# Two further, unread TensorE products per group ahead of the third layer in a message-passing kernel

## The reference

```
h = silu(rbf @ fc_w1 / sqrt(8))          # 8 -> 64
h = silu(h @ fc_w2 / sqrt(64))           # 64 -> 64
weight = h @ fc_w3 / sqrt(64)            # 64 -> 128, split into w00, w01, w10, w11
gs, gv = l1_s[edge_src], l1_v[edge_src]  # rows of a linear map of the source node
o00 = w00 * gs * sh0
o01 = w01[:, :, None] * gs[:, :, None] * sh1[:, None, :]
o10 = w10[:, :, None] * gv * sh0[:, :, None]
o11 = w11 * (einsum('ecm,em->ec', gv, sh1) / sqrt(3))
agg = segment_sum(message, edge_dst) / count
out = x + sc + tanh(alpha) * (agg @ lin2)
```

## Time and profile before

| | before |
|---|---|
| median of 3 runs | 2496.71 us |
| lowest and highest run | 2487.68 and 2497.35 us |
| span of the profiled execution | 2483.8 us |
| PE busy | 1811.4 us, 73% |
| DVE busy | 1783.0 us, 72% |
| POOL busy | 1578.4 us, 64% |
| ACT busy | 1199.1 us, 48% |
| mean granted TensorE clock | 0.826 |

### The profile page before, as it was taken

One profiled execution on the slowest core, in us unless ns is written; L12 is line 12 of the kernel. 1 busy time (PEld: TensorE's weight loads), 2 busy tenths in 40 slices (PEclk: granted clock), 3 DMA queues, 4 the chain that ended last, 5 costly groups with the idle time before them and its releaser, 6 DMA issues. The chain is left out here.

```text
span 2483.8 us, 34021 instructions
## 1 busy us (share of the span) xinstructions
PE 1811.4 (73%) x7969; PEld 1174.2 (47%) x7969; DVE 1783.0 (72%) x4669; ACT 1199.1 (48%) x3310; POOL 1578.4 (64%) x1624
## 2 busy tenths in 40 slices
PE   6577777787777777767677767667787776877777
PEld 6344444454444444444444434444554444544544
DVE  8577767767776777767676667767677776777777
ACT  6354545455454555444444344445444444445443
POOL 7566666666666666666666666666666666666563
PEclk9588878878888887788787878888888888888889
DMA  7322222222222222222122222222222222222222
GB/s 214 70 64 67 56 64 66 66 56 66 66 59 62 67 65 56 55 48 50 46 50 48 48 48 49 54 50 64 57 67 62 59 65 66 53 64 61 59 66 55
DMA packets 347699, 155.73 MB, mean 63 GB/s; under 512 B 237983, under 2 KB 322048, under 8 KB 347584
## 3 DMA queue, kind: packets, MB, share of 16 engines
q0 software_dynamic: 50016, 102.51, 15.7%
q1 hardware_dynamic: 296938, 51.75, 11.4%
q10 hardware_dynamic: 630, 0.29, 0.0%
HBM read 134.27 MB, written 20.15 MB: 62 GB/s over the span
## 5 line engine op out<-in xcount | busy, mean ns | idle before, releaser
L970 POOL DMA_INDIRECT lin_g<-lin_table,src_ix x1563 | 1530.0, 979 | 865.1 <-issue 441.5
L1157 ACT ACTIVATE lin_sh<-lin_g,harm 128x128 f32<-128x128 f32 x1563 | 483.8, 396 | 94.6 <-DMA lin_g<-lin_table,src_ix 87.6
L1040 PE MATMUL ps_sums<-near_sums,far_hot 128*128 128x257 f32 x520 | 208.0, 488 | 440.8 <-DVE agg L1474 206.0
L1030 PE MATMUL ps_near<-msg,onehot 128*64 128x257 f32 x3126 | 507.5, 471 | 1.2 <-DVE msg L1423 1.2
L1018 PE MATMUL ps_w<-w,h 128*128 128x256 f32 x1566 | 462.6, 440 | 28.2 <-ACT key_all L1167 18.5
L1018 PEld LDWEIGHTS ps_w<-w,h 128*128 128x128 f32 x1566 | 395.3, 272 | 135.4 <-issue 44.9
L999 PE MATMUL ps_h<-rbf,w 32*128 32x192 f32 x1044 | 277.0, 390 | 138.0 <-issue 67.1
L1415 DVE TENSOR_TENSOR msg<-lin_sh,key_all 128x576 f32<-128x576 f32 (+1 forms) x261 | 197.3, 756 | 249.9 <-ACT key_all L1167 209.5
L1167 ACT ACTIVATE key_all<-ps_w 128x768 f32<-128x768 f32 x261 | 213.5, 818 | 305.2 <-remote 188.6
L1030 PEld LDWEIGHTS ps_near<-msg,onehot 128*64 128x64 f32 x3126 | 241.3, 164 | 230.6 <-issue 175.7
L1383 DVE TENSOR_TENSOR lin_sh<-lin_g,ps_meta 128x576 f32<-128x576 f32 (+1 forms) x261 | 196.6, 753 | 212.2 <-DMA lin_g<-lin_table,src_ix 207.0
(11 more groups left out here) (175 smaller groups left out, 1655.2 us busy)
## 6 DMA issues: line engine op xcount, KB each, us to landing
lin_g<-lin_table,src_ix POOLq DMA_INDIRECT x1563
dist_in<-in_edge_weight SPq DMA_DIRECT2D x67, 96.0 KB
lin_table<-lin_out SPq DMA_DIRECT2D x24, 256.0 KB, 2.6
x_in<-in_x SPq DMA_DIRECT2D x24, 256.0 KB
skip_table<-x_in SPq DMA_DIRECT2D x24, 256.0 KB
xq<-in_x SPq DMA_DIRECT2D x23, 256.0 KB, 3.9
harm<-in_edge_attr SPq DMA_DIRECT2D x66, 48.0 KB
x_in<-skip_table SPq DMA_DIRECT2D x8, 256.0 KB
```

The source lines that it names most:

```text
L970: pool.indirect_dma_start(slot_tiles(s, u)[rows, t, :], None, lin_table, bass.IndirectOffsetOnAxis(ap=src_ix[rows, s.phase, u, col:col + 1 ...
L1030: mm = pe.matmul(ps_near[half * NEAR:(half + 1) * NEAR, 0:MSG + 1], onehot[:, u, t, :], msg[:, u % 2, t, :], start=(j == 0), stop=(j == PA ...
L1040: pe.matmul(ps_nodes(i), far_hot[:, u, :], near_sums[:, u % 2, :], start=True, stop=True).then_inc(sums_ready, 1)
L1157: last = act.activation(lin_sh0[:, u % 2, j, :], slot_tiles(s, u)[:, j, :], ACT.Copy, scale=harm[:, s.phase, u, harm_col(j):harm_col(j) + 1])
```

## The change

Each call of `layer3` issues two more products ahead of its own three, behind the wait for `w_copied`. Their stationary operand is `w2`, their moving operand all 256 columns of `w3`, and they write columns 768 to 1023 of `ps_w`, which nothing reads. They signal no semaphore. In the changed file the new products stand at L1018, and each later line is up to three further down (layer 3's own products L1021, `near_layer` L1033, `segment_sum` L1043).

```
+WARM = 2
...
                             at_least(pe, w_copied, i * SLOTS + u)
+                            for _ in range(WARM):
+                                pe.matmul(ps_w[:, TILES * P:], w2[:], w3[:], start=True, stop=True)
                             cols = h2[:, u % 2, :].rearrange("p (c j) -> p j c", j=PAIRS)
                             for j in range(PAIRS):
                                 mm = pe.matmul(ps_w[:, 2 * j * P:(2 * j + 2) * P], cols[:, j, :], w3[:], start=True, stop=True)
```

## The result

| | before | after |
|---|---|---|
| median | 2496.42 us | 2540.54 us |
| lowest and highest run | 2487.68, 2497.35 us | 2530.16, 2550.09 us |
| profiled span | 2483.8 us | 2540.1 us |
| mean granted clock | 0.826 | 0.864 |

The ratio is 1.018 (95% interval 1.0147 to 1.0213): slower, 44 us by the medians and 56.3 us by the two profiled spans. The forecast was 2531 us, slower by 1.4%. The medians are of four runs each.

A forecast was written before the change was run, and what follows sets the result against it. It took POOL's gathers and their waits, mostly for late TensorE messages, as the bound. Span 2483.8 plus 34 us gave 2518 us; with 12.9 us from span to median, 2531 us, range 2470 to 2630 us.

The forecast's parts named there:

- POOL's waits as the kernel's time: POOL's gathers: 1530.0 us busy plus 865.1 us idle fill nearly the whole span, so a wait there is kernel time.
- The new rows: TensorE ahead of layer 3: 4 matmul rows a call, 1044 in all, 1.18 us a group, 308 us.
- The size of the cost: Whole loop: half the upper reading for the added TensorE time, 0.13 us a group, 34 us.
- the upper slope: Loop phases with extra TensorE work: 0.14 to 0.22 us of period per added us, 43 to 68 us over 261 groups.
- the phases of the earlier trace: Three stretches of the loop before: 9.06 us a group plain, 9.13 and 9.30 with 0.49 and 1.08 us extra TensorE work.
- The clock: TensorE's mean granted clock would rise from 0.826 to 0.84 to 0.90, without making the kernel faster.
- The waits: POOL's waits for TensorE, 408 us, would grow by about 34 us; TensorE's idle before the sums would shrink, PE exceed 80% busy.
- remote: POOL's 155 waits, 325.1 us, counted as waiting for TensorE, whose messages arrived late and as POOL paused.
- "issue" pauses: POOL's 1347 short pauses of 0.33 us, 441.5 us, the cost of starting the next gather.
- The idle time before the sums: TensorE idle 440.8 us before L1040; the new products would fill 100 to 250 us of it.
- The rival "exposed": DVE's 113 waits at L1415 for ACT's copy each grow 1.18 us: 133 us, 2630 us in all; chance 0.14.
- The rival "hidden": New products end inside TensorE's idle time before L1040, POOL's waits stay: 2490 to 2509 us; chance 0.22.

The follow-up runs named there:

- drain: Kernel before plus a POOL wait, ahead of each group's first gather, until the previous group's six gathers have landed: ratio 1.0848, 2702.1 us.
- drain_half: Kernel before plus a POOL wait for the previous group's gathers to land, at every second group only: ratio 1.0315 to before.
- in_gap: The change's two products (255 columns each) moved behind layer 3, between TensorE's two waits of the sums: ratio 1.0088 to before.
- thin_gap: Kernel before plus four products of only 4 columns a group, behind layer 3 between TensorE's two waits of the sums: ratio 1.012.
- thin: Four products of only 4 columns a group ahead of layer 3, in place of the change's two of 256: ratio 1.0379 to before.
- at_sums: The change's two products (255 columns each) moved behind layer 3 and behind both waits of the sums: ratio 1.0177 to before.
- l3first: Kernel before, no added products, with layer 3 issued ahead of layers 1 and 2 in each step: ratio 0.9999.
- unpaced: Kernel before without POOL's waits ahead of the third and fifth gather of a group, which protect no data: ratio 1.0294.

## Why the prediction was right

- **POOL's waits as the kernel's time.** This step was taken from the rows of before and was not isolated by any run. That POOL's idle time grew with the span shows nothing (see the result). That its schedule matters is shown: drain and drain_half delay POOL alone and cost 8.5% and 3.15%. That the change acts through POOL's waits is argued, and next to it stands the way over layer 3 and DVE.
- **The new rows.** 1044 rows and 308 us were forecast; 1044 and 334.0 us were measured.
- **The size of the cost.** This is the mis-sized term: 34 us, or 0.13 us a group. It measured 44 us by the medians, 0.17 us a group, and 56.3 us by the profiled spans, 0.22 us a group. I had halved the upper slope because ACT and DVE also got work in the phases of the earlier trace rows; the slopes as read, 0.17 to 0.26 us a group, hold both. The halving was the wrong step, if a small one. That the slopes fit is partly luck: by the experiments the cost of a microsecond depends on where it stands and what it is made of, and the skip rows and finished blocks stand elsewhere.
- **The clock.** Forecast 0.84 to 0.90, measured 0.864. That its return doesn't turn the sign was right. What the prediction did not see is how much it may be: in the change's place nearly the same time without columns costs 3.8% in place of 1.8%, while in the gap the difference is 0.3 points. The Trainium skill, page "TensorE: Matmul & The Clock Gate", section "Why this matters for your kernels", advises keeping TensorE busy so that its clock stays up; the runs agree as to the clock, and show that the added time costs more than the clock gives.
- **The waits.** POOL's waits (remote, L1040 or L1043, L1008 or L1009) went from 407.7 to 436.4 us, +29 where about 34 was forecast. That agreement is no proof, since the span grew by 56.3 us, about twice as much; of the rest, 15.5 us are "issue" pauses of POOL (441.5 to 457.0 us) that the prediction took as fixed. The idle time before the sums fell by 135 us, inside 100 to 250. TensorE stands at 78% busy, not above 80%: its other rows were shorter, and neighbouring rows overlap.
- **The rival "exposed"** had DVE's wait at L1415 growing by 133 us and 2630 us as the time. The wait grew by 112 us, and the time is far below. Its condition was that the wait ahead would not shrink by as much: that shrank by 77 us, so 35 us are left, near the 44 us of the cost. In full this rival is refuted. In part it is not: in_gap against after, and thin_gap against thin, cost half and a third with layer 3 left alone. Against it speak at_sums and l3first, each with a second change of its own.
- **The rival "hidden"** holds in part: in_gap halves the cost by moving the products into TensorE's wait.

Open are how the change's cost parts between a later layer 3 and later sums, what delays TensorE's messages while POOL gathers, and why unpaced is slower. A kernel that delays layer 3 as after does, and the sums not at all, would decide the first. No version beats the kernel before.

## What to carry to other kernels

In a ring of engines, an idle time that grows with the span singles out no engine: each one whose work is unchanged shows it. A wait that grows on one engine may also have moved from the wait ahead of it. What tells causes apart is to move the added work and to look, for each place, at both what it delays and which idle time it fills; at_sums changed both at once, and its equal cost proved less than it seemed to. Here the same products cost half when they stood inside a wait that TensorE had anyway and delayed no copy. Further products left TensorE's clock higher, but never paid for their own time in the kernel before.

## What the runs showed of the hardware

The kind of the added rows made more difference to the granted clock than their number. With four thin products a group, 2088 rows in 292.6 us, it was 0.836 (0.826 before); with as many rows of 256 columns in 589.2 us it was 0.894, and with half of them in 334.0 us 0.864. With 1040 rows of 255 columns behind layer 3, in at_sums, it was 0.883.

A thin product of 4 columns held TensorE more than half as long as one of 256: to the end of layer 3, four thin ones a group took 0.95 us more than none at full clock, two of 256 columns 0.86 us.

ACT waited up to 6.4 us at a time, 342.1 us in all, at the near sums' copy for messages of TensorE whose rows had ended by the trace. With a wait for the landing at each group `near_ready` changed 0.21 us after TensorE's rows in the mean in place of 2.29 us. The ends of TensorE's rows are modelled, so whether the rows or only their messages end late is open.
